# Softmax in a fused token, mixer and attention kernel: unscaled probabilities into the transposes, their sums by a product with ones, the scaling at the exit from PSUM

## The reference

```
q, k, v = (xp @ w_qkv) split into 12 heads of 16
a = softmax(q k^T * hd**-0.5, axis=-1)        # 274 queries x 274 keys, per head
o = a v                                        # 274 x 16 per head
o = o @ w_proj + b_proj
```

## Time and profile before

| | |
|---|---|
| median of 3 runs | 6137.19 us (6126.9 to 6150.05) |
| profiled execution, first to last instruction (span) | 6123.8 us |
| the profiled execution's time outside the span | not given; the median is 13.4 us above the span |
| busy: TensorE, VectorE, ScalarE | 5309.5, 5554.8, 3780.6 us |
| DMA, HBM | 53 GB/s over the span |
| chain of waits by engine | PE 40%, DVE 33%, issue 20%, ACT 6% |

### The profile page before, as it was taken

The page is one execution under the profiler, slowest core; times in us unless marked ns, Lnnn a source line. Parts: engine busy times, 40 slices in busy tenths (PEclk is TensorE's granted clock), DMA queues, the critical chain, the costliest instruction groups (busy, mean ns, idle before and its releaser), DMA issues.

```text
span 6123.8 us, 74116 instructions
## 1 busy us (share of the span) xinstructions
PE 5309.5 (87%) x22816; PEld 3509.9 (57%) x22816; DVE 5554.8 (91%) x6069; ACT 3780.6 (62%) x9506; POOL 0.8 (0%) x8
## 2 busy tenths in 40 slices
PE   5788888888888888888889999888998989989888
PEld 3555555555555555555556655655656556556554
DVE  6999999999999999999999999998999989999962
ACT  3566666656666556666666666666666666666643
POOL 0000000000000000000000000000000000000000
PEclk7898888888888888888989988898888888889885
DMA  3211211211211211211221111111111212112100
GB/s 101 64 45 57 64 45 53 66 51 51 64 52 46 66 58 44 65 53 44 65 65 42 60 60 38 64 58 44 64 45 54 66 37 65 50 47 65 40 23 2
DMA packets 56934, 327.85 MB, mean 54 GB/s; under 512 B 13246, under 2 KB 15742, under 8 KB 23627
## 3 DMA queue, kind: packets, MB, share of 16 engines
q1 hardware_dynamic: 56490, 322.53, 16.6%
HBM read 313.52 MB, written 8.98 MB: 53 GB/s over the span
## 4 chain that ended last, share of the span: by engine, by line
PE 40%; DVE 33%; issue 20%; ACT 6%; DVEq 1%; DMA 0%; SPq 0%; ACTq 0%
DVE hs L953 12%; PE y_ps L417 10%; PE f_ps L530 7%; DVE hs L936 4%; PE f_ps L542 4%; DVE hs L957 4%; PE f_ps L581 3%; PE f_ps L496 2%; PE a_ps L455 2%; DVE neg_max L1062 2%; DVE xc L1016 2%; PE f_ps L511 2%; PE f_ps L592 2%; PE f_ps L487 2%; PE a_ps L465 1%
## 5 line engine op out<-in xcount | busy, mean ns | idle before, releaser
L953 DVE TENSOR_TENSOR_SCAN hs<-decay,hs 128x2192 f32<-128x2192 f32 x384 | 1811.1, 4717 | 28.0 <-issue 19.7
L417 PE MATMUL y_ps<-hs,ident 128*128 128x274 f32 x5376 | 1719.8, 455 | 89.5 <-issue 31.3
L715 ACT ACTIVATE decay<-dt,inner_s 128x273 f32<-128x273 f32 x3072 | 1380.6, 513 | 75.7 <-issue 40.3
L417 PEld LDWEIGHTS y_ps<-hs,ident 128*128 128x128 f32 x5376 | 1104.1, 217 | 480.8 <-issue 187.8
L936 DVE TENSOR_TENSOR hs<-b_rows,dtu 128x2192 f32<-128x2192 f32 x384 | 935.5, 2436 | 99.2 <-PE y_ps L417 76.7
L957 DVE TENSOR_TENSOR hs<-hs,c_rows 128x2192 f32<-128x2192 f32 x384 | 934.7, 2434 | 3.4
L530 PE MATMUL f_ps<-qk 16*92 16x274 f32 x2304 | 733.5, 458 | 227.9 <-ACT hid L788 216.4
L805 ACT ACTIVATE hid<-f_ps 92x273 f32<-92x273 f32 (+1 forms) x1152 | 421.7, 393 | 556.6 <-PE f_ps L542 552.4
L788 ACT ACTIVATE hid<-f_ps,neg_max 92x274 f32<-92x274 f32 x1152 | 544.0, 480 | 301.1 <-DVE neg_max L1062 300.9
L530 PEld LDWEIGHTS f_ps<-qk 16*92 16x92 f32 x2304 | 350.7, 174 | 549.2 <-ACT hid L788 344.6
L542 PE MATMUL f_ps<-ident,hid 92*92 92x92 f32 x3456 | 514.7, 286 | 86.8 <-ACT hid L805 48.7
(11 more groups left out here) (103 smaller groups left out, 5773.8 us busy)
## 6 DMA issues: line engine op xcount, KB each, us to landing
b_rows<-bc_rows SPq DMA_DIRECT2D x128, 1096.0 KB, 5.6
c_rows<-bc_rows SPq DMA_DIRECT2D x128, 1096.0 KB, 5.6
xp<-in_patches SPq DMA_DIRECT2D x32, 588.0 KB, 7.4
out<-h SPq DMA_DIRECT2D x32, 205.5 KB, 2.2
bc_rows<-bc_s SPq DMA_DIRECT2D x64, 34.2 KB, 1.5
h<-in_txt SPq DMA_DIRECT2D x32, 57.8 KB, 2.3
w_in_s<-in_w_in SPq DMA_DIRECT2D x1, 1152.0 KB
fc_s<-in_fc SPq DMA_DIRECT2D x2, 576.0 KB
```

Of the source, the lines that this page charges most:

```text
L417: mm = pe.matmul(y_ps[:, 0:T], ident[:, :], hs[q % 2][:, n, :], start=(q % 2 == 0 and n == 0), stop=(q % 2 == 1 and n == end - 1))
L715: e = act.activation(decay[half][:, n, t], dt[d][:, u, t], ACT.Exp, scale=inner_s[:, d, u, s:s + 1])
L953: dve.tensor_tensor_scan(i, a, i, 0.0, ALU.mult, ALU.add).then_inc(scan_done, 1)
```

## The change

Exp no longer takes its row sums, and nothing divides the probabilities before they are turned. `turn` waits only for the Exp. Behind a group's 12 value products, 12 more products of the same shape multiply `prob_t` by `ones_v` (92 x 32 ones, row 0 of tiles 1 and 2 zeroed as in `v_mask`) into bank 4; so partition 32r + i of bank 4 holds head r's sum for each query, for every i. ScalarE takes Ln of it and Exp with scale -1 (`invert_sums`), in place of `av_copy`, and VectorE multiplies bank 3 by the result on its way to `o_s` (`av_scale`), in the gap after. `AV_GAPS` are 18, 23, 28 instead of 19, 24, 29.

```diff
-        row_sum = sb("row_sum", [QT, 2, 3])
-        row_inv = sb("row_inv", [QT, 2, 3])
+        ones_v = sb("ones_v", [QT, 3, 32])
+        key_inv = sb("key_inv", [128, T])
...
-        AV_GAPS = (19, 24, 29)
+        AV_GAPS = (18, 23, 28)
...
+            pool.memset(ones_v[:, :, :], 1.0).then_inc(s_cp, 1)
+            pool.wait_ge(s_cp, 5)
+            pool.memset(ones_v[0:1, 1:3, :], 0.0).then_inc(s_cp, 1)
...
             def turn(f, hd, lo, hi):
-                pe.wait_ge(p_norm if lo == 0 else p_norm_last, at(f, HEADS, hd + 1))
+                pe.wait_ge(pexp, at(f, 3 * HEADS, 3 * hd + hi))
...
                 mm.then_inc(av_mm, 1)
+                for k in range(3):
+                    for r in range(4):
+                        mm = pe.matmul(f_ps[32 * r:32 * r + 32, 4, 0:T], ones_v[:, k, :], prob_t[:, r, k, :],
+                                       start=(k == 0), stop=(k == 2), skip_group_check=True)
+                mm.then_inc(sum_mm, 1)
...
                     act.activation(prob[hd % 2][:, t, :], f_ps[0:QT, t, 0:T], ACT.Exp, scale=-1.0,
-                                   bias=neg_max[:, hd % 2, t:t + 1], accum_out=row_sum[:, hd % 2, t:t + 1])\
-                        .then_inc(pexp, 1)
-
-            def normalise_last(f, hd):
-
-                act.wait_ge(inv_done, at(f, HEADS, hd + 1))
-                act.activation(prob[hd % 2][:, 2, :], prob[hd % 2][:, 2, :], ACT.Copy,
-                               scale=row_inv[:, hd % 2, 2:3]).then_inc(p_norm_last, 1)
+                                   bias=neg_max[:, hd % 2, t:t + 1]).then_inc(pexp, 1)
...
                 if hd % 4 == 0 and lo == 0:
-                    wait(act, av_mm, at(f, GROUPS, hd // 4))
+                    wait(act, sum_mm, at(f, GROUPS, hd // 4))
...
-            def av_copy(f, g):
-                act.wait_ge(av_mm, at(f, GROUPS, g + 1))
-                if g == 0:
-                    wait(act, pr_mm, at(f, 1, 0))
-                act.activation(o_s[:, g, :], f_ps[:, 3, 0:T], ACT.Copy).then_inc(av_copied, 1)
+            def invert_sums(f, g):
+                act.wait_ge(sum_mm, at(f, GROUPS, g + 1))
+                wait(act, av_copied, at(f, GROUPS, g))
+                act.activation(key_inv[:, :], f_ps[:, 4, 0:T], ACT.Ln).then_inc(sum_ln, 1)
+                act.wait_ge(sum_ln, at(f, GROUPS, g + 1))
+                act.activation(key_inv[:, :], key_inv[:, :], ACT.Exp, scale=-1.0).then_inc(sum_inv, 1)
...
-            def normalise(f, hd):
-                s = hd % 2
-                dve.wait_ge(pexp, at(f, 3 * HEADS, 3 * hd + 3))
-                wait(dve, p_norm_last, at(f, HEADS, hd - 1))
-                dve.reciprocal(row_inv[:, s, :], row_sum[:, s, :]).then_inc(inv_done, 1)
-                dve.wait_ge(inv_done, at(f, HEADS, hd + 1))
-                for t in range(2):
-                    a = dve.tensor_scalar(prob[s][:, t, :], prob[s][:, t, :], row_inv[:, s, t:t + 1], None, ALU.mult)
-                a.then_inc(p_norm, 1)
+            def av_scale(f, g):
+                dve.wait_ge(av_mm, at(f, GROUPS, g + 1))
+                dve.wait_ge(sum_inv, at(f, GROUPS, g + 1))
+                if g == 0:
+                    wait(dve, pr_mm, at(f, 1, 0))
+                dve.tensor_tensor(o_s[:, g, :], f_ps[:, 3, 0:T], key_inv[:, :], ALU.mult).then_inc(av_copied, 1)
...
-                if gap - 1 in SCORE_GAPS:
-                    normalise(f, SCORE_GAPS.index(gap - 1))
+                if gap - 1 in AV_GAPS:
+                    av_scale(f, AV_GAPS.index(gap - 1))
```

More of the change, by code:

```diff
@@ L250, in build @@
         pexp = sem("prob_exp")
-        inv_done = sem("inv_done")
-        p_norm = sem("prob_normed")
-        p_norm_last = sem("prob_last_tile_normed")
+        sum_mm = sem("sum_mm")
+        sum_ln = sem("sum_ln")
+        sum_inv = sem("sum_inverted")
         pt_mm = sem("prob_t_mm")
@@ L678, in front @@
                 pe.wait_ge(s_w, 16 * len(LOADS))
-                pe.wait_ge(s_cp, 4)
+                pe.wait_ge(s_cp, 6)
                 pe.wait_ge(s_c, CONSTS)
@@ L838, in fine_mid @@
                 if gap in TURN_GAPS:
-                    normalise_last(f, TURN_GAPS.index(gap))
                     turn_copy(f, TURN_GAPS.index(gap), 0, 2)
@@ L852, in fine_late @@
                 if gap in AV_GAPS:
-                    av_copy(f, AV_GAPS.index(gap))
+                    invert_sums(f, AV_GAPS.index(gap))
                 if gap in FC1_GAPS:
@@ L896, in front @@
                 act.wait_ge(s_w, 16 * len(LOADS))
-                act.wait_ge(s_cp, 4)
+                act.wait_ge(s_cp, 6)
                 act.wait_ge(s_c, CONSTS)
@@ L1201, in front @@
                 dve.wait_ge(s_c, 14)
-                dve.wait_ge(s_cp, 4)
+                dve.wait_ge(s_cp, 6)
                 dve.tensor_tensor(centre_w[:, 0, :], ident[0:CH, 0:CH], mean_w[:, :], ALU.subtract).then_inc(s_c, 1)
```

## The result

Before 6132.05 us (median of four, 6120.72 to 6150.05), changed 6424.88 us (6417.91 to 6472.73): ratio 1.0486, 95% interval 1.0439 to 1.0534. Slower, as forecast, but by 293 us and not by 82; the range ended at 6290. The profiled execution spans 6416.1 us at a mean granted clock of 0.861 (before 6123.8 and 0.874).

What follows compares the result with a forecast made beforehand. It took TensorE to be late in three stretches of each image's attention, VectorE between them. An extra 2.4 us an image (74 us for 31) and 8 for the last gave 6123.8 + 13.4 + 82 = 6219 us, range 6060 to 6290.

Steps and rivals of the forecast that it cites:

- the clock term: First and third TensorE stretches: 0.8 us an image added for a slow first group, 1.8 credited for regained clock.
- the load term: TensorE's three stretches: 8.35 us an image of added ones, copy waits and third group, less idle time that vanishes.
- Ones, 1.6 us a group: Behind each group's value products: twelve ones products cost the same as those, 1.6 us, three times an image, 4.8 us.
- Copy waits, 0.65 us each: Gaps 18, 23, 28: TensorE waits for ScalarE's copy of the group's last tile, 0.65 us each, 1.95 an image.
- The clock credit of 1.8 us an image: First and third stretches: 3.6 of 28 slow us turn to 2.4 GHz as TensorE stands less, worth 1.8 us.
- rival A: Fuller TensorE queues regain the high clock in the attention: 5950 us in full, 6062 in the milder case; chance 0.22.
- Idle time that can vanish, 4.95 of 6.15 us: TensorE's idle time in its three stretches, 6.15 us an image, absorbs added load; 1.2 us of it stays.
- The third group brought ahead of the y sum, 1.6 us: Last stretch: the third group's value products move ahead of the y sum that frees L936, putting 1.6 us on the chain.
- VectorE 8.0 us less an image: VectorE loses 9.5 us of inverses and scalings, gains 1.5; only about six of twelve pairs stand where it leads.
- C: Ones products not packed beside each other, 6.3 us a group instead of 1.6: 6656 us; chance 0.05.
- B: VectorE's six leading inverse-and-scale pairs, 4.8 us an image, cancel TensorE's extra work: no change, 6137 us; chance 0.18.
- The signs I had named: If right: TensorE busy above 5400 us, minima waiting for scores behind gap 18, L936 in gap 30 some 2.4 us later.

Runs made afterwards that it cites:

- m1: Kernel before with only the first group's value products a gap earlier (AV_GAPS 18, 24, 29): 6290.36 us, ratio 1.0258.
- c2: m1 plus one unread product put where TensorE waits for ScalarE's last copy, ahead of the value products: 6143.09 us, ratio 1.0019.
- c4: m1 plus one unread product behind the first group's value products, where TensorE does not wait: 6308.38 us, ratio 1.0304.
- e3: Kernel before with only the earlier place of all three groups of value products (AV_GAPS 18, 23, 28): 6466.22 us, ratio 1.0538.
- m3: e3 with the moved value products issued behind the in-projection of the same gap instead of ahead of it: 6297.57 us, ratio 1.0272.
- e1: Kernel before without the inverse, the scalings and the accumulator reads, probabilities not divided at all: 6048.28 us, ratio 0.9854.
- c3: Kernel before with only the third group moved (gap 28), plus eight unread products ahead of gap 32's mean products: 6157.66 us, ratio 1.005.
- w3: Changed kernel with value and ones products behind the in-projection, third group left in gap 29 behind the y sum: 6127.69 us, ratio 1.0002.
- w5: e1 with 6, 2 and 3 unread products ahead of the scores of heads 1, 3 and 11: 5911.49 us, ratio 0.9639.
- w2: Kernel before with 6, 2, 1, 1, 2 unread products ahead of the scores of heads 1, 3, 9, 10, 11: 6072.19 us, ratio 0.9913.
- w4: w3 with unread products: 6, 2, 2 ahead of scores of heads 1, 3, 11, five ahead of the fourth mean products: 6038.30 us, 0.9845.
- v1: Kernel before with the division folded into the transposes, as products by diagonal matrices of the inverse sums: 6246.59 us, ratio 1.0185.

## Why the prediction was right in sign and wrong in size

The sum had two kinds of terms. Load was 8.35 - 4.95 = 3.4 us an image, the clock 0.8 - 1.8 = -1.0; together 2.4. Between the two spans the kernel lost 292 us, 9.4 an image. The low level took (1 - 0.861) x 6416.1 - (1 - 0.874) x 6123.8 = 120 us more of TensorE's time than before, 3.9 an image. As an estimate, which takes all of this as time of the chain, load and order are left with 172 us, 5.5 an image. So the clock term is off by 4.9 us and of the wrong sign, the load term is short by 2.1. The sign of the whole was not luck: the load that the sum named is there, in gap 29 above all.

*Ones, 1.6 us a group.* Right: 1.57 at full clock, 167.5 us for 96. The Trainium skill ("TensorE: Matmul & The Clock Gate", Part 3) gives no factor for four column tiles; its factor for four row tiles, which the prediction took, would have made 2.06 (an estimate), and the trace does not agree with that for four strips of 32 columns.

*Copy waits, 0.65 us each.* Right as idle time: 46.5 us in 96, 0.48 each, 66.4 by the weight loads. Wrong as a price: the first alone cost 164 us in m1, 5.3 us an image, and c2 against c4 shows that nearly all of it comes with the low clock behind the wait. The prediction also held that the first two groups "stay within their stretch". The second does not: gaps 23 and 24 lose 72 us, 2.3 an image, at the full clock.

*The clock credit of 1.8 us an image.* This is the step that failed, by its sign: with the 0.8 for the slow first group it makes -1.0 an image, and the traces have +3.9. I read a low clock in the first and third stretch and let denser TensorE work earn some of it back; but the move put a new idle time in front of the one stretch that ran at 1.00. e3, m1, m3, c2 and c4 say it five ways. What I cited for rival A from the Trainium skill ("TensorE: Matmul & The Clock Gate", "Why this matters for your kernels": gaps between bursts bring the lower clock) points the right way, and I used it only for gaps that go, never for the gap that the change adds. But the page speaks of gaps much longer than the 0.48 us of c2 and c4; that so short a wait can do it stands in these runs alone.

*Idle time that can vanish, 4.95 of 6.15 us.* Wrong, and the second step that failed. The stalls for L1072, 2.47 us at L542 among them, went, but the transposes' idle time rose all the same, from 86.8 to 108.5 us in the two kernels' groups: 106.6 of it is now for the copy L806, which in gap 27 stands behind the silu and its two table loads on ScalarE (L751 to L753):

```profile
2044.60 1.28 ACT L753 ACT_TABLE_LOAD   x1
2045.90 0.39 ACT L806 ACTIVATE hid<-f_ps 92x273 f32<-92x273 f32 x1
```

The timeline of TensorE in the changed kernel, gaps 27 to 32:

```profile
2046.34 0.44 PE L545 MATMUL f_ps<-ident,hid 92*92 92x92 f32 x3 [2.37 <-ACT hid L806]
...
2055.67 1.59 PE L554 MATMUL f_ps<-hid,v_s 92*32 92x274 f32 x24 [0.48 <-ACT hid L806]
2057.08 1.57 PE L560 MATMUL f_ps<-hid,ones_v 92*32 92x274 f32 x24
2058.58 0.72 PE L482 MATMUL a_ps<-dt_lo,dt_w_s 13*128 13x274 f32 x2
2059.24 1.19 PE L420 MATMUL y_ps<-hs,ident 128*128 128x274 f32 x4
...
2070.54 3.17 PE L499 MATMUL f_ps<-res,centre_w 96*96 96x274 f32 x8 [3.71 <-DVE res L1080]
```

*The third group brought ahead of the y sum, 1.6 us.* Mechanism right, size short: 0.48 + 1.59 + 1.57 = 3.64 us now precede L420 at 2059.24, which frees VectorE's L937. (The new scaling on VectorE ends there too: the y sum ends 0.14 us and VectorE's own work 0.09 us ahead of L937 in 30 of the 31 images, so a shorter queue on one of the two alone would have brought next to nothing. The forecast took the y sum for the later one.) Gap 29 grew by 4.6: the other 1.0 us I take for a part of the 2.1 that VectorE had saved in gaps 25 to 28 and that ends in this wait (in e1, which moves nothing, gap 29 is 1.5 us longer). And a second price I had not seen: TensorE then runs dry, 3.71 us ahead of L499, and the products behind it run at 1.2 GHz (3.17 us for what took 2.09 in an image at full clock). Gaps 32 and 33 lose 73 us in the changed kernel, and c3's fillers give back 66 there; w3 puts the whole place of the third group at 107.

*VectorE 8.0 us less an image.* Instructions as forecast (41.7 us for 96 scalings, 434 ns, between the two bounds); busy 5355.1, not 5295: 18.8 of the 60 are longer minima, the rest is in no group's row (before, some records of the scaling ran beside their neighbours', so taking them out took less off the busy time than off the sum). *It leads only in part*: e1's 77 us bear that out, and w5's 161 say that a part of what is missing there goes to the waits and the low clock behind them.

*Rivals.* C fell by the row of L560. B took TensorE's extra as paid by VectorE's saving; w3, another order, is where that came true (1.0002). A is in part what happened, turned round: the clock moved, against the change. The signs I had named came: TensorE busy above 5400 (5555.9, of which the slow clock is a part), new waits of the minima behind gap 18 (318.4 us in all) and a later L936 in gap 30 (5.2 us behind gap 14 in images 3 to 15, where 2.4 were forecast); the clock of the middle stretch was not on my list, and should have headed it.

Open: why some images keep the full clock behind the same wait (m1) and others don't; why the waits of 0.48 us ahead of the second and the third group leave gaps 23, 24, 29 and 30 at 1.00 in the changed kernel; and how the 76 us of the ones outside gaps 23, 24 and 29 divide between their own time and the clock.

## What to carry to other kernels

Where the granted clock stands at its high level, a change that adds even a short wait of TensorE (0.48 us here) ahead of a dense stretch can cost that stretch's length at 1.2 GHz and not the idle time: take that price as the upper bound (here it was paid behind the first group and not behind the other two), and put work that is ready into the wait, or, if there is none, products that nobody reads. Price the order too: what is queued ahead of the product that another engine waits for costs its full length even at the full clock (gaps 23, 24 and 29). Cut an image at the bounding engine's instructions and compare gap by gap, with clock and idle time in each: it showed in one table what the totals hid. And when the load of an engine falls, look for the next place where it waits for another, for there the saving ends.

## What the runs showed of the hardware that I had not expected

- Twelve products that nobody reads, put into waits of every image, made the kernel before 54 us faster (w2, 0.9913) and fifteen the changed one, in w3's order, 89 us (w4 against w3), although TensorE executes more. The mean granted clock rose from 0.874 to 0.901 and from 0.889 to 0.913.
- One 0.57 us product in a wait of 0.48 us was worth 165 us in 31 images against the same product behind the wait, 5.3 us each (c2, c4). The same 0.48 us ahead of the second group of the changed kernel brought no low clock (gaps 23 and 24 at 1.00).
- A float32 product by a diagonal matrix is two passes, a transpose one: 6912 instructions of 272 ns against 3456 of 286 (v1). With the products in their place gaps 24 to 26 of images 3 to 15 run at the full clock, where they had it for 56%, 64% and 4% of the time before; whether the products or the waits that went with the third tile's scaling do this was not run apart.
- 24 instructions of 92 x 32 by 274 columns, in four column strips, take 1.57 to 1.59 us at full clock and 2.97 at the low one: as many us as 6 instructions of 128 x 128 by 274 (1.58 in the earlier trace rows).
